# Causal attention between two mixture feed-forwards on one core: the value product in three slots of a group instead of five

## What is computed

```python
x = x + 0.5 * ffn(layernorm(x))
x = x + attn(layernorm(x))
x = x + 0.5 * ffn(layernorm(x))
# attn, 16 heads of 8 features, per batch
scores = einsum('bhqd,bhkd->bhqk', q, k) / sqrt(8) - (m * rel)   # ALiBi slopes
scores = where(causal_mask, scores, -inf)
out = einsum('bhqk,bhkd->bhqd', softmax(scores), v)
# ffn, 8 experts of which the best 2 count, and a shared gated expert
```

## Time and profile before

| | us |
|---|---|
| median of 3 runs | 324.27 |
| lowest, highest | 324.04, 324.76 |
| the profiled execution | 322.91 |
| its span (first to last instruction) | 320.8 |
| TensorE busy in the span | 286.1 |
| VectorE busy | 253.4 |
| ScalarE busy | 171.5 |
| GpSimd busy | 124.4 |

### The profile page before, as it was taken

How to read it: one execution, slowest core, us unless ns; L and a number is a source line. 1 busy time by engine, 2 the same in 40 slices (tenths; PEclk the granted TensorE clock), 3 DMA queues, 4 the chain that set the end, 5 groups by cost and what they waited for, 6 DMA issues and landing times.

```text
span 320.8 us, 7148 instructions
## 1 busy us (share of the span) xinstructions
PE 286.1 (89%) x2328; PEld 185.2 (58%) x2328; DVE 253.4 (79%) x1061; ACT 171.5 (53%) x326; POOL 124.4 (39%) x253
## 2 busy tenths in 40 slices
PE   0398998998995998999899999999999999999994
PEld 0387886996762534334343344233444798889894
DVE  4459899788999688897969989999621698988775
ACT  2233234432422678875878978787888343324330
POOL 0367243605134145547315533484733342420200
PEclk9999999999999579998999999999999999999999
DMA  6820000362031014421104411110000001000011
GB/s 179 217 34 1 2 0 4 121 199 76 1 135 65 1 54 148 144 62 52 40 15 149 150 53 54 53 53 4 4 2 3 0 2 33 2 11 25 1 33 35
DMA packets 20668, 17.73 MB, mean 55 GB/s; under 512 B 2460, under 2 KB 19420, under 8 KB 20572
## 3 DMA queue, kind: packets, MB, share of 16 engines
q1 hardware_dynamic: 19912, 17.05, 17.7%
q10 hardware_dynamic: 720, 0.23, 0.3%
HBM read 9.74 MB, written 7.34 MB: 53 GB/s over the span
## 4 chain that ended last, share of the span: by engine, by line
PE 58%; DVE 19%; issue 7%; POOL 7%; ACT 4%; DMA 2%; SPq 1%; DVEq 0%; POOLq 0%; ACTq 0%
PE bank L841 14%; PE bank L971 10%; PE bank L939 8%; PE bank L779 7%; DVE X L638 6%; PE bank L780 5%; PE bank L781 5%; DVE masked_s L706 4%; POOL probs L373 2%; DVE stats L575 2%; PE bank L912 2%; DMA X<-in_x 2%; PE bank L981 2%; ACT probs L483 2%; PE bank L994 1%
## 5 line engine op out<-in xcount | busy, mean ns | idle before, releaser
L706 DVE CUSTOM_DVE_ANT_0 masked_s<-bank,causal_sb 128x512 f32<-128x512 f32 (+3 forms) x256 | 109.8, 486 | 13.5 <-PE bank L912 13.2
L483 ACT ACTIVATE probs<-bank 128x512 f32<-128x512 f32 x160 | 89.8, 602 | 28.3 <-PE bank L939 27.4
L638 DVE SCALAR_TENSOR_TENSOR X<-bank,coef,X 128x128 f32<-128x128 f32 x288 | 80.7, 343 | 21.1 <-PE bank L841 14.6
L841 PEld LDWEIGHTS bank<-w_sb,act 128*128 128x128 f32 x512 | 67.8, 193 | 5.9
L841 PE MATMUL bank<-w_sb,act 128*128 128x128 f32 x512 | 68.1, 276 | 0.0
L373 POOL TENSOR_SCALAR_AFFINE_SELECT probs<-probs 128x512 f32<-128x512 f32 x64 | 39.8, 635 | 68.5 <-ACT probs L483 68.5
L912 PE MATMUL bank<-KA,QA 54*128 54x512 bf16 (+3 forms) x256 | 59.1, 318 | 6.9 <-DVE smax L706 6.0
L422 ACT ACTIVATE act<-bank 128x512 f32<-128x512 f32 x72 | 41.8, 594 | 40.2 <-PE bank L781 40.2
L939 PE MATMUL bank<-QA,KA 57*128 57x128 bf16 (+3 forms) x256 | 59.2, 317 | 0.2
L971 PE MATMUL bank<-probs,VA 128*32 128x256 f32 (+2 forms) x640 | 52.8, 399 | 1.4 <-issue 0.9
L779 PE MATMUL bank<-XH,w_hi 128*128 128x512 f32 x88 | 42.8, 486 | 4.9 <-DVE gated L623 2.3
(11 more groups left out here) (83 smaller groups left out, 320.2 us busy)
## 6 DMA issues: line engine op xcount, KB each, us to landing
qk_scratch<-qk_parts SPq DMA_DIRECT2D x8, 384.0 KB, 2.6
QA<-qk_scratch SPq DMA_DIRECT2D x32, 96.0 KB, 2.2
KA<-qk_scratch SPq DMA_DIRECT2D x32, 96.0 KB, 2.3
qk_scratch<-qk_parts SPq DMA_DIRECT2D x8, 256.0 KB, 2.9
qk_scratch<-qk_parts SPq DMA_DIRECT2D x8, 128.0 KB, 2.8
QA<-smaxT SPq DMA_DIRECT2D x64, 3.0 KB
out_x<-X SPq DMA_DIRECT2D x4, 256.0 KB, 2.3
X<-in_x SPq DMA_DIRECT2D x3, 256.0 KB, 6.6
```

Of the source, the lines that this page charges most:

```text
L483: nc.scalar.activation(dst, src, ACT.Exp).then_inc(exp_done, 1)
L638: m = nc.vector.scalar_tensor_tensor(X[:, b * NT + t, :], Y_BANK[i % 3][:, t * P:(t + 1) * P], coef[:, j % 2, t, n:n + 1], X[:, b * NT + t ...
L706: r = nc.vector.tensor_tensor_reduce(masked_s[:, u % 4, off:off + n], bank[:, off:off + n], causal_sb[:, S - n:S], 1.0, -3e38, ALU.add, AL ...
L841: m = nc.tensor.matmul(Y_BANK[i % 3][:, r], a, w2_sb[:, n, :], start=True, stop=True)
```

## The change

The first two pieces, which belong to one key tile, become one of 512 columns in slot 2. The piece of 384 columns moves from slot 6 to slot 5, behind that of 128. Slots 3 and 6 have none any more. There are 16 matmuls a group instead of 20, over as many columns.

```diff
-            PIECES = ((0, 0, 256), (0, 256, 512), (3, 384, 512), (1, 128, 512), (2, 256, 512))
-            PIECE_SLOTS = (2, 3, 5, 6, 8)
+            PIECES = ((0, 0, 512), (3, 384, 512), (1, 128, 512), (2, 256, 512))
+            PIECE_SLOTS = (2, 5, 5, 8)
...
-                    if i in PIECE_SLOTS and 0 <= n - 1 < NGT:
-                        weigh_values(n - 1, PIECE_SLOTS.index(i))
+                    if 0 <= n - 1 < NGT:
+                        for k, slot in enumerate(PIECE_SLOTS):
+                            if slot == i:
+                                weigh_values(n - 1, k)
```

## The result

The change makes the kernel **slower by 0.6%**: 326.0 us in the median of 20 runs (323.2 to 329.3) against 324.3 us (20 runs, 322.0 to 327.2); ratio 1.0063, 95% interval 1.0039 to 1.0087. The ratio and its interval leave out the slowest executions of either kernel (over 1.5% above its fastest), the medians do not. The forecast was 323.9 in a range up to 325.6, no change that can be told.

What follows compares the result with a forecast made beforehand. TensorE or VectorE was taken to bound the attention steps, varying by step. Gains in TensorE-paced steps less delays and bubbles summed to -0.4 us, forecast as 323.9 us against the 324.27 median, range 321.2 to 325.6.

Steps and rivals of the forecast that it cites:

- rival 3: Longer wait before L779 brings one more episode of lowered TensorE clock, some 1.5 us: 325.4 us; chance 0.09.
- Cost of a piece: Value product on TensorE: 0.15 us of each piece is fixed; the 512-column piece was taken at 1.00 us.
- Term 2: 512-column piece in slot 2: 0 on TensorE, -0.15 us in step 15 alone; scores of slot 3 0.43 us late.
- The queue behind the smaxT copy: Late slot 3 scores delay smaxT and L779 by 0.43 us in step 6; steps 6 to 8 together +0.2.
- Term 1: Two pieces adjacent in slot 5: -0.24 us in each step that TensorE paces.
- Step 4: -0.5 us: -0.24, and 0.26 from slot 3's piece moved ahead by a slot, running at 2.4 GHz.
- The bubbles: VectorE waits before slot 6 in steps 3 and 10 to 12: 0.16 us each, +0.6 in all.
- Rival 2: Slower through the smaxT loop, with DMA wait before slot 0's scores beyond 0.8 us and VectorE idle: 325.7 us; chance 0.15.

Runs made afterwards that it cites:

- the additions: Extra matmuls leaving results unchanged: in the first feed-forward and step 0, changed kernel 322.92 us; in steps 3, 5, 10, 12, changed kernel 321.95 us.
- all additions: Kernel before plus extra matmuls at the first feed-forward's end and in steps 0, 3, 5, 10, 12: 319.61 us, ratio 0.9865.
- the merge alone: Kernel before with only the first two pieces merged into 512 columns in slot 2, 384-column piece left in slot 6: 324.57 us, ratio 1.0028.
- the pair: Kernel before with only the 384-column piece moved to slot 5 behind the 128-column one, five pieces kept: 325.22 us, ratio 1.0040.

## Why the prediction was wrong

**The step that failed is rival 3**, the clock, held at 0.09 because "in the trace steps 5 to 16 show no such fall"; the sum leaves it out but for the 0.26 of step 4. One profiled execution cannot show how often a thing occurs that varies from run to run, and this one was among the quarter of runs with the highest clock, 0.973 against 0.964 in the mean: its 322.91 us lay 1.4 below the median, which I noted as a difference between execution and median and did not ask about. The change lowers the mean clock by 0.0065, worth 1.6 of its 2.3 us. That this is a cause, the additions show: with the later episodes gone the change fell from 326.5 to 322.0 us, and with the first stretch gone too the two kernels are equal. The rest comes by the half clock too, in another way: the sum costs step 1 as if at full clock, though a stretch at 0.50 reached into it in the trace before (to 116.6 us), and there the longer piece costs 0.85.

**The sum was -0.4 us, and at full clock it measures +0.06 +- 0.39.** Without the 0.26 that step 4 was to gain by the clock it is -0.17, inside that interval, but by luck: its terms are off by up to 0.7 and cancel. By the profiles with all additions (us; step 3 stands in two terms of the sum, 0.0 and 0.15):

```
steps       1      2, 3   4      5, 9, 13   6 to 8   10 to 12   14     15     sum
forecast    +0.19  +0.15  -0.24  -0.72      +0.20    +0.45      +0.19  -0.39  -0.17
measured     0.00  +0.06  +0.05  +0.02      +0.49    +0.08      -0.03  -0.56  +0.11
```

The additions themselves stand in steps 3, 5, 10 and 12, so that these are not quite the steps of the kernels without them. The terms:

- *Cost of a piece*: right. 1.00 taken, 0.99 measured. The count of records was a slip, 16 matmuls in each of 16 groups make 512 records, as measured, not 480.
- *Term 2*, nothing gained in slot 3: right, 208.61 - 207.86 = 0.75 in the earlier trace rows against 153.97 - 153.65 = 0.32 after.
- *The queue behind the smaxT copy*: right in place, and for a single wait in size. L779 in step 6 waited 0.60 as forecast, and step 14 has +0.42 from the merge alone, for 0.43. But steps 6 to 8 together lose 0.49, more than twice the 0.2.
- *Term 1, -0.24 in each step that TensorE paces*: the most mis-sized term. With both halves steps 5 and 9 gave 0.05 each and step 13 lost 0.12, where 0.24 each was forecast. The rows for L988, in slot 9 of these steps, show why. In step 5 it waits 1.50 us for `XL` of VectorE (L583), in the kernel before and after the change alike (rows below), so TensorE did not pace that step. In step 9 it now waits 0.15 for `normalise` (DVE AO), and before the change it did not wait for VectorE: `normalise` stands behind the maxima of slot 7, and these VectorE begins no earlier, its slot 6 having come late. TensorE's own list of work was shorter, but the transposes at its end belong to VectorE's pace. Only in steps 14 and 15, in which VectorE has no maxima, does the pair gain, 0.47 and 0.41, and that is more than 0.24.
- *Step 4*, -0.5 with 0.26 from a piece moved ahead of the fall of the clock: meaningless as a term. The whole episode was elsewhere in the next execution.
- *The bubbles*: the 0.16 before slot 6 is in the profile, and so is a wait for the DMA beyond 0.8 us. Rival 2 wanted VectorE idle there as well, and it is not. Steps 10 to 12 together lose 0.08 in the kernels with additions, against 0.45.

L988 in step 5, before and after the change:

```profile
160.72 0.63 PE L988 MATMUL bank<-id_f,AO 128*128 128x128 f32 x4 [1.50 <-DVE XL L583]
```

```profile
160.22 0.63 PE L988 MATMUL bank<-id_f,AO 128*128 128x128 f32 x4 [1.50 <-DVE XL L583]
```

Why the pair leads to more episodes was not settled, only that they begin around the steps where it leaves slots 6 and 7 without value work while TensorE waits for VectorE in slots 0 to 2.

## What to carry to other kernels

Where runs of a kernel differ by a per cent, ask for the granted clock of each before costing a change from one trace; groups of times can be different lengths of time at half clock. Then look for the places in which TensorE has little to do. Work that nobody needs, put there, bought 1.3% here from an already tuned program, more than any order of the pieces; and orders should be compared only with the clock held up, since a better order (the pair) can lose its gain to it.

## What the runs showed of the hardware

TensorE's clock fell to half for 3.4 us (143.9 to 147.3 in the trace before) or 6.8 (223.3 to 230.1 in the second profile of the change), behind places in which TensorE waited. The longest single wait in the 10 us ahead of these two falls was 0.57 and 0.77 us; ahead of the fall at 161 us in the profiles of the change it was 1.50, and ahead of the long stretch in the trace before 1.33. The same 1.50 us wait stands at the end of step 5 in the profile before, and no fall follows there. In the later episodes of the kernels shown, TensorE reads as 100% busy, so a busy share does not tell them; the clock column does. The stretch at the beginning of the attention, 13.7 to 20.5 us, began at 99 to 103 us and went on although TensorE was busy for most of it (in the trace before all but one of the microseconds from 103 to 116 read 0.97 or more): in step 0 it has scores and a projection of values, but no value product. With the added matmuls at the end of the first feed-forward and in step 0 it never began; which of the two is needed was not tried. The Trainium skill, "TensorE: Matmul & The Clock Gate", part "A second HAM failure mode", has short idles between groups of matmuls as such a cause, and these runs agree with it. Without the half clock the kernel before takes 4.7 us less, the additions' own time included (means of 324.2 and 319.5).
